# A two-layer AdaLN transformer stack on one core: where ScalarE's function tables are asked for, and a new order of the steps and idle matmuls of its two streams

## The chip, the cores and the metric

The kernel runs on 1 of the 8 cores of one Trainium2 chip. The metric is the device time of one execution in microseconds (us), lower is better; the number compared is the median of several executions. Engines: PE is TensorE, ACT is ScalarE, DVE is VectorE, POOL is GpSimd, and SP (SyncE) issues every DMA.

## The reference, cut to what matters

Eight sequences of 256 tokens with 128 features pass through two blocks, each with an attention part and a feed-forward part; each part gets `layernorm(x) * (1 + c) + s` and is added to `x` behind a gate.

```
x += ga * L0_attn(h)  # 8 heads of 64; an indexer picks 96 of 128 keys per half; Exp, Ln
x += gb * L0_ffn(h)   # two layers: windowed attention (l2norm, softmax) and a Gelu MLP of 341
x += ga * L1_attn(h)  # 16 heads of 8 over 256 keys; softmax
x += gb * L1_ffn(h)   # 16 experts, top 8 by a sigmoid router, one shared expert; Silu
```

All arithmetic is float32 but for the one-hot gathers, which are bf16 products.

## The kernel before

Sequences are worked on in pairs: stream 0 has sequences 0, 2, 4, 6 and stream 1 has 1, 3, 5, 7, four rounds each. Each engine has one Python generator per stream (`tensor_stream`, `scalar_stream`, `vector_stream`, `pool_stream`, `sync_stream`), cut into steps by `yield`. A step is mostly one wait on a semaphore and the few instructions that it releases. The two generators of an engine are merged into one instruction queue by a string of `STEPS_IN_TURN`: each character is a number in base 36, so many steps of one stream, the next character so many of the other, in turn. An engine works off its queue in order, so a step that waits holds up all behind it, of both streams.

`BUSY` has one string per stream, with a base-36 digit for each call of `keep_busy` in `tensor_stream`: so many idle matmuls (bf16, 128 columns of weights by 256, line L530, on the constant `mean_mat`) go ahead of the wait there, into a PSUM region whose contents are not needed. They compute nothing.

ACT needs a function table. Exp and Ln share one table set (`LN_AND_EXP`), Gelu and Silu have others; Copy, Identity, Square, Relu and Abs run with any. `table(act, name)` (L1149 to L1156) issues a load if the name differs from the last name asked for in build order: `preload_act_table_set` (L1153) for Ln and Exp, `preload_act_table` (L1155) for Gelu and Silu. Before the change a step function asks once, as a rule at the end of the step that precedes the one that uses the table, so ahead of a `yield`; between the asking and the use the string may place steps of the other stream. If the table that is then resident lacks the function of an activation, the compiler puts a load of its own right ahead of it; the trace lists such a load under the line of the activation (L1412 is the Exp of windowed attention, L1465 the Exp of the 16-head attention, L1519 the Silu of the experts).

Other lines named below: L616 the transposes of the probabilities (they wait for `u_prob`, which DVE sends after L1567 or L1570), L795 the down products of the experts, L2027 the product of Silu and up part on DVE, L1782 the cast that sends `top_ready`, L456 and L458 the saves of the picked indices, L467 their broadcast back to all partitions into `idxb`, L474 and L482 the save and the return of the gathered scores, L490 the store of the output.

Of the kernel before, what the change touches and what calls it, by code (L numbers as in the profile page):

```python
# [49 lines left out]
def shape_constants():  # L50
# [47 lines left out]
    "pe": ("922122242242e26437657223435346132423112621738272f3a16124132a5c6525522g83c2a9a4632a3c2a62281622232224241112221212"  # L98
            "3341135152514113315421252525252322235172663764314223236349143432249481c3a5226223622837254a3a161241525234c5c48362"
            "2837254a481228232224241112221212334113515231213112415411133215252523222351726637821243422123334934326435a4c3a3a1"  # L100
            "612415282c4a5226223622837254a5248362283c2a6127122823222424111222121233411351525151312231253515252523222252726637"
            "6532662372341734579381c3a4216423622w1628224322142421522z0i837252a62281622232224241112221212334113411231213112114"
            "5153d"),
    "act": ("d27253411927554275536143217325233323134311226132642184322823354581123226523431246822342622354622332g42e453333113"
            "5153552374c555552j573213423553416496262236434122911275541523221325534a43228253147862243325534741142h42e453333113"
            "51235233237452721145552j57454235b4633143285343634334327584322825334a61323221325534781224332543124622322h42e45333"
            "31135153722353545575552i411745423553415433752422368422712285543426132i222112452486222r53125534522332g42e45334442"
            "35236592c"),
    "dve": ("z0e4f69445494a4a79341444545412711436143315643163419221117252165518422164381521557174225951155917422a315541442121"
            "2mz082335e5385b375c358256441351e311b4c7834144454568415391544d123917424222112531557164127252165514452264182531557"  # L110
            "1641283411454144422mz131835c3228l355c358256441351d4a4f7834144494541245371641943421535174725216551a21251111623315"
            "21557164122752531557184312153111454144422mz0813153321a125354119365c358256441351c4b4f7834144454465113311436184491"
            "63917422521234121q5655214452122z0125114571542141631554144422mr131533c55385l"),
    "pool": ("gg11hhii44i243731m11hhii44e2838p11hhii44k2238p11hh922g744823339"),
    "sp": ("6211261131422611314226113142282"),
}
BUSY = [("a0g0v10000000000000000200b0010j00000000000500a00408000030d000140448000003000000000000000004006001b0001a780000630"
         "001000049f000063013000404480000030000000030000600000035g200000a70000000000000a000a0000630b0000404480000006000000"
         "03000010100006000b0091a701000000000001000000000301370e0000000006"),
        ("000000q00b00000000000400010000f03004063000000a006400000300351e0000000000030000e0097000e0020003080000a00000000000"  # L120
         "80000a002d80000301370e0000000000030001e0000000090000030001000203j000063090000a004240000301370e0006000000030004e0"
         "000000e00000030b0000o1k3l000000000500o1k3l5000848f00004044800000")]
# [170 lines left out]
def program(nc, A, out, idx_scratch, score_scratch):  # L293
    ctx = ExitStack()
    with ctx:
# [862 lines left out]
        def scalar_stream(act, st, s):  # L1158
# [12 lines left out]
            def ln_rstd(n):  # L1171
                table(act, LN_AND_EXP)
                yield
                act.wait_ge(*at("ln_var", n + 1))
                last_ = st.mark(act.activation(m.rstd, bank[2][:, 0:L], ACT.Ln, bias=eps_col[:, :]))
                yield
                st.wait(last_)
                act.activation(m.rstd, m.rstd, ACT.Exp, scale=-0.5).then_inc(*one("ln_rstd"))
# [7 lines left out]
            def query_parts(k):  # L1186

                q_abs, q_mu = m.q_tmp[k][0:2]
                raw = bank[3][:, H * DC:]
                table(act, LN_AND_EXP)  # L1190
                yield
                act.wait_ge(*at("q2_mm", k + 1))
                if k == 1:
                    act.wait_ge(*at("isummed", 1))
                last_ = st.mark(act.activation(q_abs, raw, ACT.Abs))
                yield
                st.wait(last_)
                last_ = st.mark(act.activation(q_abs, q_abs, ACT.Exp, scale=-1.0))
                yield
                st.wait(last_)  # L1200
                act.activation(q_mu, raw, ACT.Relu)
                act.activation(q_abs, q_abs, ACT.Ln, bias=one_col[:, :]).then_inc(*one("q2_log"))
                lat = bank[3][:, 0:256].rearrange("p (h n) -> p h n", h=H)
                copy(m.qa[k][:, :, 0:DC], lat)
                copy(m.qb[k][:, :, 0:DC], lat).then_inc(*one("q_latent"))
# [48 lines left out]
            def rescale(l, k):  # L1254
                table(act, LN_AND_EXP)
                yield
                act.wait_ge(*at("ssq_ready", 2 * l + k + 1))
                last_ = st.mark(act.activation(rs[s][:, k, :], ssq[s][:, k, :], ACT.Ln, scale=LN_SHIFT))
                yield
                st.wait(last_)  # L1260
                act.activation(rs[s][:, k, :], rs[s][:, k, :], ACT.Exp, scale=-0.5, bias=shift_col[:, :]).then_inc(*one("rs_ready"))
# [11 lines left out]
            for r in range(ROUNDS):  # L1273
# [24 lines left out]
                table(act, LN_AND_EXP)  # L1298
# [4 lines left out]
                yield  # L1303
                act.wait_ge(*at("kr_abs", 1))
                last_ = st.mark(act.activation(m.kr_abs, m.kr_abs, ACT.Exp, scale=-1.0))
                yield
                st.wait(last_)
# [29 lines left out]
                for i in range(6):  # L1337
                    yield
                    if i == 5:
                        act.wait_ge(*at("xg_turned", 1))  # L1340
                        act.wait_ge(*at("pdiag_zero", 1))
                        for t in range(GP):
                            part = slice(RANKS * t, RANKS * t + RANKS)
                            ins = copy(m.pdiag[part, :, t, :], bank[1][part, 0:H * NG].rearrange("p (h j) -> p j h", j=NG))
                        ins.then_inc(*one("pdiag_ready"))
                    if i >= 2:
                        u = i - 2
                        yield
                        act.wait_ge(*at("u_pv", u + 1))
                        copy(m.oTa[:, u % 2, cols(u // 2)], bank[3][:, 0:P]).then_inc(*one("u_out"))  # L1350
                    if i < 4:
                        T, half = i // 2, i % 2
                        table(act, LN_AND_EXP)
                        yield
                        act.wait_ge(*at("u_bias", i + 1))
                        for h in range(4):
                            probs = m.probs_a[T][:, 4 * half + h, :]
                            ins = act.activation(probs, probs, ACT.Exp, bias=nb[s][:, i, h:h + 1], scale=SCALE_A,  # L1358
                                                 accum_out=ls[s][:, i, h:h + 1])
                        ins.then_inc(*one("u_exp"))  # L1360
                    if 0 < i < 4:
                        yield
                    if 0 < i < 5:
                        yield from turned_out(0, i - 1, m.PTa[(i - 1) % 2])
                    yield
# [8 lines left out]
                for l in range(2):  # L1374
                    table(act, LN_AND_EXP)
# [16 lines left out]
                    for i in range(6):  # L1392
# [10 lines left out]
                        if i < 4:  # L1403
                            T, half = i // 2, i % 2
                            n = keys(T)
                            table(act, LN_AND_EXP)
                            yield
# [18 lines left out]
                    table(act, ACT.Gelu)  # L1426
                    for c in range(3):
                        n = HC[c]
                        yield
                        if c != 1:  # L1430
                            act.wait_ge(*at("f_g", 2 * l + 1 + c // 2))
# [23 lines left out]
                for v in range(4):  # L1455
                    yield
                    if v == 2:
                        act.wait_ge(*at("x_pv", 1))
                        copy(m.o1[:, 0:L], bank[0][:, 0:L]).then_inc(*one("x_o"))
                        yield  # L1460
                    table(act, LN_AND_EXP)
                    yield
                    act.wait_ge(*at("st_mm", v + 1))
                    for q in range(4):
                        act.activation(m.PT1[v][:, q, :, :].rearrange("p j n -> p (j n)"), bank[q], ACT.Exp, scale=SCALE_1)\  # L1465
                           .then_inc(*one("st_exp"))
                        if q == 1:
                            yield
                yield
                act.wait_ge(*at("x_pv", 2))  # L1470
                copy(m.o1[:, L:], bank[0][:, 0:L]).then_inc(*one("x_o"))
                yield
                table(act, LN_AND_EXP)
                yield
                act.wait_ge(*at("x_sum", 1))
                last_ = st.mark(act.activation(m.rs1, bank[1], ACT.Ln))
                yield
                st.wait(last_)
# [5 lines left out]
                yield  # L1484
                table(act, LN_AND_EXP)
                yield
# [3 lines left out]
                table(act, ACT.Silu)  # L1490
                copy(m.x_res, bank[3][:, P:3 * P].rearrange("p (k n) -> p k n", k=NT))
                copy(m.gate_row, bank[3][:, 3 * P:]).then_inc(*one("x_res"))
                yield
                act.wait_ge(*at("e_gate", 1))
                act.activation(m.moe_g[:, 0:L], bank[0][:, 0:L], ACT.Silu).then_inc(*one("e_silu"))
                yield
                for i in range(1, 6):
# [14 lines left out]
                    if i < 5:  # L1512
                        table(act, ACT.Silu)
                        for j in range(2):
                            yield
                            act.wait_ge(*at("e_gate", 2 * i + j))
# [767 lines left out]
```

## Time and profile before

| | |
|---|---|
| median of 3 runs | 1498.68 us (1488.72 to 1499.29) |
| the profiled execution | 1503.2 us, its span 1501.4 us |
| busy: PE, DVE, ACT, POOL | 1292.5, 900.6, 897.6, 362.2 us (86, 60, 60, 24%) |
| mean granted TensorE clock | 0.950 |

The span goes from the first to the last instruction; 1.8 us of the profiled time lie around it. Busy time of PE includes the idle matmuls.

### The profile page before, as it was taken

What the parts mean: (1) busy time and instruction counts of PE and PEld (TensorE: products, weight loads), DVE (VectorE), ACT (ScalarE), POOL (GpSimd) and SP (SyncE); (2) the same over time, 40 slices, a digit from 0 to 9 for tenths busy, and PEclk for the clock granted to TensorE, in tenths of its full rate; (3) what the DMA queues carried; (4) which work ended last, traced back from release to release, by engine and by line L of the source; (5) the groups of instructions that cost most, each with busy time, mean ns of one, the idle gap of its engine ahead of it and who ended that gap; (6) DMA issues with size and microseconds to landing.
All of it is one profiled execution on the core that took longest, in us unless ns stands there. A gap on an engine that the chain in (4) does not pass through costs nothing.

```text
span 1501.4 us, 31001 instructions
## 1 busy us (share of the span) xinstructions
PE 1292.5 (86%) x11954; PEld 914.2 (61%) x11954; DVE 900.6 (60%) x2920; ACT 897.6 (60%) x2256; POOL 362.2 (24%) x580
## 2 busy tenths in 40 slices
PE   7788988879887998988898988887899798988887
PEld 5455655657764665656665655665676566656566
DVE  3966665553776666663476566756367566656533
ACT  3435676647843677747673567764785356665463
POOL 0601242000450222210153023310036123040003
PEclk8898999999999999999998999999999989999999
DMA  8120000000022000000012100000002200000000
GB/s 281 51 77 13 2 1 1 1 5 4 5 65 76 4 2 1 1 1 4 8 47 70 28 2 1 1 1 5 5 5 64 71 10 2 1 1 1 1 1 8
DMA packets 31795, 34.90 MB, mean 23 GB/s; under 512 B 19168, under 2 KB 23712, under 8 KB 31136
## 3 DMA queue, kind: packets, MB, share of 16 engines
q1 hardware_dynamic: 31648, 32.92, 7.4%
q8 instruction: 95, 1.56, 0.4%
q14 instruction: 52, 0.43, 0.1%
HBM read 25.46 MB, written 7.44 MB: 22 GB/s over the span
## 4 chain that ended last, share of the span: by engine, by line
PE 56%; ACT 21%; DVE 14%; issue 3%; DMA 3%; POOL 2%; SPq 2%; POOLq 0%; DVEq 0%; ACTq 0%
ACT arena L1412 4%; PE ps L530 4%; PE ps L557 4%; PE ps L795 4%; ACT arena L1164 4%; DVE small L1953 3%; PE ps L728 3%; ACT L1153 2%; PE ps L687 2%; PE ps L1069 2%; PE ps L616 2%; PE ps L1052 2%; PE ps L772 2%; PE ps L780 2%; PE ps L657 2%
## 5 line engine op out<-in xcount | busy, mean ns | idle before, releaser
L1164 ACT ACTIVATE arena<-ps 128x512 f32<-128x512 f32 (+7 forms) x560 | 258.6, 483 | 283.2 <-PE ps L580 39.1
L530 PE MATMUL ps<-mean_mat 128*128 128x256 bf16 x1120 | 157.0, 282 | 19.9 <-ACT arena L1164 10.1
L2101 POOL TENSOR_TENSOR arena<-arena 128x512 f32<-128x512 f32 x64 | 80.8, 1272 | 313.7 <-DVE arena L1604 312.4
L530 PEld LDWEIGHTS ps<-mean_mat 128*128 128x128 bf16 x1120 | 107.7, 101 | 63.2 <-issue 29.3
L1412 ACT ACTIVATE arena<-arena,small 128x128 f32<-128x128 f32 (+1 forms) x256 | 129.7, 509 | 13.2 <-DVE small L1890 12.8
L1579 DVE CUSTOM_DVE_ANT_0 arena<-ps,mask_w_bf 128x128 f32<-128x128 f32 (+1 forms) x256 | 67.5, 319 | 64.3 <-PE ps L671 63.8
L1953 DVE TENSOR_REDUCE small<-ps 128x4 f32<-128x1024 f32 x64 | 75.5, 1220 | 30.2 <-PE ps L1052 29.7
L795 PE MATMUL ps<-w_experts,arena 128*128 128x128 f32 x544 | 77.1, 299 | 11.2 <-DVE arena L2027 11.0
L795 PEld LDWEIGHTS ps<-w_experts,arena 128*128 128x128 f32 x544 | 71.6, 210 | 24.0 <-issue 11.8
L2027 DVE TENSOR_TENSOR arena<-arena,ps 128x512 f32<-128x512 f32 x64 | 43.0, 686 | 71.4 <-ACT arena L1519 40.2
L1358 ACT ACTIVATE arena<-arena,small 128x224 f32<-128x224 f32 (+1 forms) x128 | 56.3, 444 | 42.1 <-DVE small L1838 42.1
L1465 ACT ACTIVATE arena<-ps 128x512 f32<-128x512 f32 x128 | 66.3, 601 | 25.2 <-PE ps L1088 25.1
L557 PE MATMUL ps<-hot_ring,arena 128*96 128x512 bf16 x192 | 58.0, 447 | 23.8 <-DVE gath L1814 21.7
L1814 DVE TENSOR_TENSOR gath<-ps,rank_tab 96x512 f32<-96x512 f32 x96 | 62.8, 681 | 25.2 <-PE ps L557 18.0
L1567 DVE TENSOR_TENSOR arena<-arena,small 128x512 f32<-128x512 f32 x96 | 70.6, 736 | 2.8
L2186 POOL TENSOR_TENSOR arena<-arena 128x256 f32<-128x256 f32 x32 | 24.1, 754 | 196.8 <-ACT arena L1507 194.9
L772 PE MATMUL ps<-arena,w_experts 128*128 128x256 f32 x272 | 69.3, 397 | 0.0
L780 PE MATMUL ps<-arena,w_experts 128*128 128x256 f32 x272 | 66.1, 383 | 1.7 <-ACT arena L1507 1.5
L728 PE MATMUL ps<-w_wqkv,arena 128*128 128x512 f32 x128 | 62.5, 631 | 3.7 <-DVE arena L1557 3.7
L616 PE MATMUL ps<-packed,arena 128*128 128x128 f32 x384 | 62.9, 288 | 3.0 <-DVE arena L1570 1.3
L1579 DVE CUSTOM_DVE_ANT_0 arena<-ps,mask_a_bf,small 128x192 f32<-128x192 f32 (+1 forms) x128 | 41.6, 381 | 38.6 <-PE ps L603 38.2
L1507 ACT ACTIVATE arena<-ps,arena 128x128 f32<-128x128 f32 x128 | 36.5, 371 | 46.3 <-PE ps L795 46.3
(291 smaller groups left out, 2965.9 us busy)
## 6 DMA issues: line engine op xcount, KB each, us to landing
idxb<-idx_scratch SPq DMA_DIRECT2D x24, 512.0 KB, 5.3
score_scratch<-arena SPq DMA_DIRECT2D x96, 64.0 KB, 1.7
w_experts<-in_experts SPq DMA_DIRECT2D x3, 1088.0 KB, 16.3
w_wqkv<-in_wqkv SPq DMA_DIRECT2D x1, 1536.0 KB, 9.4
arena<-score_scratch SPq DMA_DIRECT2D x96, 16.0 KB, 2.0
arena<-in_x SPq DMA_DIRECT2D x8, 128.0 KB, 2.2
out_x<-arena SPq DMA_DIRECT2D x8, 128.0 KB, 1.8
packed<-in_packed SPq DMA_DIRECT2D x2, 503.0 KB, 4.0
```

The costliest lines, as they stand in the source:

```text
L530: mm(to, still[:, 0:P], still, start=True, stop=True)
L557: last = mm(bank[g % 2][0:GF, :], m.kv_part[i][:, 0, :], hot[n][:, part], start=(i == 0), stop=(n < 2 and i == 2))
L616: last = pe.transpose(bank[2][:, cols(h)], probs[:, h, :], ident[:, :])
L728: mm(bank[2 * k + j], m.sh[:, cols(k)], wqkv[:, l, 512 * j:512 * j + 512], start=True, stop=True)\
L772: last = mm(bank[j // 2][:, L * (j % 2):L * (j % 2) + L], experts[:, 0, e, :], m.hT, start=True, stop=True)
L780: last = mm(to[:, L * (j % 2):L * (j % 2) + L], experts[:, 1, e, :], m.hT, start=True, stop=True)
L795: last = mm(bank[2 + j // 2][:, 256 * (j % 2) + P * k:256 * (j % 2) + P * k + P], m.moe_h[:, L * j + P * k:L * j + P * k + P], experts[:, ...
L1164: return act.activation(dst, src, ACT.Copy)
L1412: ins = act.activation(probs, probs, ACT.Exp, bias=nb[s][:, i, h:h + 1], scale=cqs[s][:, T, hh_:hh_ + 1], accum_out=ls[s][:, i, h:h + 1])
L1579: ins = dve.tensor_tensor_reduce(masked[:, h, 0:n], bank[h % 2][:, n * (h // 2):n * (h // 2) + n], mask, 1.0, least(h), ALU.add, ALU.max, ...
L1953: st.mark(dve.tensor_reduce(to, src, AX.X, ALU.max))
L2101: ins = pool.tensor_tensor(own, own, turned, ALU.add)
```

## The change

Three things are changed. `table` is asked for in each step that uses it, behind that step's `yield` and ahead of its wait, and again in each later step of the same function. The strings of `STEPS_IN_TURN` are new for all five engines (the steps themselves and their number are the same: 2138 on PE, 1841 on ACT, 2410 on DVE, 560 on POOL, 82 on SP). The strings of `BUSY` are new.

```diff
-    "pe": ("922122242242e26437657223435346132423112621738272f3a16124132a5c6525522g83c2a9a4632a3c2a62281622232224241112221212"
+    "pe": ("821112244222g26437677323236617321212244113t1a3a5841528171a455a4632a372a4522362121d672a15222846222112222424411212"
...
-    "act": ("d27253411927554275536143217325233323134311226132642184322823354581123226523431246822342622354622332g42e453333113"
+    "act": ("d212437327322a9274312464634322162623338122m23338262536488223426223348327221b27223345522ef33321313343545523344421"
...
-    "sp": ("6211261131422611314226113142282"),
+    "sp": ("621126113131112611314226113142282"),
...
-BUSY = [("a0g0v10000000000000000200b0010j00000000000500a00408000030d000140448000003000000000000000004006001b0001a780000630"
+BUSY = [("b0h50z000000000010003000050475004000000000000000000000b00000000i0000000000000000000000001000300005020000c0000000"
...
             def ln_rstd(n):
+                yield
                 table(act, LN_AND_EXP)
-                yield
                 act.wait_ge(*at("ln_var", n + 1))
                 last_ = st.mark(act.activation(m.rstd, bank[2][:, 0:L], ACT.Ln, bias=eps_col[:, :]))
                 yield
+                table(act, LN_AND_EXP)
                 st.wait(last_)
...
-                            table(act, LN_AND_EXP)
                             yield
+                            table(act, LN_AND_EXP)
                             act.wait_ge(*at("u_bias", 4 * l + i + 5))
...
-                    table(act, ACT.Gelu)
                     for c in range(3):
                         n = HC[c]
                         yield
+                        table(act, ACT.Gelu)
...
                         if q == 1:
                             yield
+                            table(act, LN_AND_EXP)
...
-                table(act, ACT.Silu)
                 copy(m.x_res, bank[3][:, P:3 * P].rearrange("p (k n) -> p k n", k=NT))
                 copy(m.gate_row, bank[3][:, 3 * P:]).then_inc(*one("x_res"))
                 yield
+                table(act, ACT.Silu)
...
-                        table(act, ACT.Silu)
                         for j in range(2):
                             yield
+                            table(act, ACT.Silu)
```

The same move is made in `query_parts`, `rescale`, the front (`kr_abs`), the softmax of the first attention, `x_rs` and the router.

## Rows read from the trace of the kernel before

**Rows 1.** The page: the chain that ended last, shares of the span by engine.

```profile
PE 56%; ACT 21%; DVE 14%; issue 3%; DMA 3%; POOL 2%; SPq 2%; POOLq 0%; DVEq 0%; ACTq 0%
```

**Rows 2.** The chain by line, shares; then its first and last table load (start, us).

```profile
by line: ACT arena L1412 4.4%; PE ps L530 4.1%; PE ps L557 4.0%; PE ps L795 3.8%; ACT arena L1164 3.6%; issue 3.2%; DVE small L1953 2.8%; PE ps L728 2.7%; ACT L1153 2.5%; PE ps L687 2.3%; PE ps L1069 2.2%; PE ps L616 2.2%; PE ps L1052 2.1%;
...
196.42 1.28 ACT L1155
...
1456.38 1.28 ACT L1153
```

**Rows 3.** Groups by line, ACT: count, busy us, mean ns, idle before.

```profile
L1155 ACT ACT_TABLE_LOAD x44 | 56.5, 1283 | 0.8
L1153 ACT ACT_TABLE_LOAD x43 | 55.2, 1283 | 0.8
L1412 ACT ACT_TABLE_LOAD x5 | 6.4, 1283 | 0.1
L1465 ACT ACT_TABLE_LOAD x3 | 3.8, 1283 | 0.1
L1519 ACT ACT_TABLE_LOAD x3 | 3.8, 1283 | 0.1
```

**Rows 4.** The chain in order of time (start, us), experts beside 16-head attention.

```profile
344.93 1.28 ACT L1155
...
346.23 0.60 ACT arena L1519
...
346.84 1.28 ACT L1465
...
348.13 1.08 ACT arena L1465 x2
...
349.24 1.28 ACT L1519
...
352.00 3.76 PE ps L795 x16
...
362.33 1.98 PE ps L795 x16
```

**Rows 5.** Groups by line, PE: the idle matmuls.

```profile
L530 PE MATMUL ps<-mean_mat 128*128 128x256 bf16 x1120 | 157.0, 282 | 19.9 <-ACT arena L1164 10.1 <-ACT arena L1243 6.0 <-DVE arena L1589 3.8
```

**Rows 6.** The chain, last round: packs of idle matmuls (start, us).

```profile
1276.68 2.79 PE ps L530 x24
...
1286.16 2.40 PE ps L530 x21
...
1329.24 5.29 PE ps L530 x24
```

**Rows 7.** Instructions of DVE in order of time, beside those packs.

```profile
1276.71 0.69 DVE L1567 TENSOR_TENSOR arena<-arena,small 128x512 f32<-128x512 f32 x1
...
1287.32 0.42 DVE L1570 TENSOR_TENSOR arena<-arena,small 128x256 f32<-128x256 f32 x1
...
1327.81 1.75 DVE L1567 TENSOR_TENSOR arena<-arena,small 128x512 f32<-128x512 f32 x1
```

**Rows 8.** Windows: stretch, length, busy of PE, PEld, DVE, ACT, POOL; clock, DMA.

```profile
345.50:352.30 6.80, 3.76 (x28) 2.76 (x27) 1.38 (x2) 6.71 (x8) 0.00 (x0) 0.93 0.01 2
352.30:359.20 6.90, 6.90 (x27) 6.25 (x27) 1.22 (x4) 5.58 (x12) 0.72 (x1) 0.57 0.00 0
```

**Rows 9.** Instructions in order of time: DVE's cast, SP's queue, round 1.

```profile
443.67 0.18 DVE L1782 CAST arena<-arena 128x64 bf16<-128x64 uint32 x1
...
444.42 2.47 SPq L482 DMA_DIRECT2D arena<-score_scratch  x4
446.93 1.58 SPq L456 DMA_DIRECT2D idx_scratch<-arena  x1
...
450.27 1.29 SPq L467 DMA_DIRECT2D idxb<-idx_scratch  x3
```

**Rows 10.** SP's queue: output stores and later broadcasts.

```profile
808.19 1.29 SPq L467 DMA_DIRECT2D idxb<-idx_scratch  x3
...
783.72 0.39 SPq L490 DMA_DIRECT2D out_x<-arena  x1
...
1142.50 0.39 SPq L490 DMA_DIRECT2D out_x<-arena  x1
```

More of the change, by code:

```diff
@@ L97 @@
 STEPS_IN_TURN = {
-    "pe": ("922122242242e26437657223435346132423112621738272f3a16124132a5c6525522g83c2a9a4632a3c2a62281622232224241112221212"
[L99 to L103, printed above, removed]
@@ L104 @@
-    "act": ("d27253411927554275536143217325233323134311226132642184322823354581123226523431246822342622354622332g42e453333113"
[L105 to L113, printed above, removed]
@@ L114 @@
-    "pool": ("gg11hhii44i243731m11hhii44e2838p11hhii44k2238p11hh922g744823339"),
-    "sp": ("6211261131422611314226113142282"),
-}
-BUSY = [("a0g0v10000000000000000200b0010j00000000000500a00408000030d000140448000003000000000000000004006001b0001a780000630"
[L118 to L122, printed above, removed]
+    "pe": ("822112244222g26437677323236617321212244113t1a3a5841528171a455a4632a372a4522362121d672a15222846222112222424411212"
+            "221212212132115142113111123125531224212523272221217272643767732323661732121224411221f1c1a2a5841528171a3611281612"
+            "31225151a452a1a1612413272a45252512282824272211123212222231114211515251511122212515152525232222527266376773232366"
+            "17321212245321z021218282112229482c1k1612413272a351a321818413272a452525122828232224141122121232431152515142115111"
+            "2221251515252523222252726236855743234349141222231112312231a1c3c584632a371a5558425682c3c1816222352h672f1a28232624"
+            "21121222121221111211211341134115351515335"),
@@ new lines @@
+    "act": ("d212437327322a9274312464634322162623338122m23338262536488223426223348327221b27223345522ef33321313343545523344421"
+            "35a2235442182c5542a52464634322162623338142i22231382625364a22111282421132228252322a21334822332l42j433445351536233"
+            "421134553233352j573212311234312464634322162623338142n2332222364f2a2322a21334d422322623334822332g321332g321134153"
+            "53546233421134553233352l55321342b43564433328233334623152a2335822172322334882224162723353317h46223a2lf43423333445"
+            "2334253a225"),
@@ new lines @@
+    "dve": ("t4o1b89645494c4369441444544652431e341441p361c41c571c442395117571744236134a1c5715412541444242412ju151335c35583523"
+            "85d3m9213833434b4e44681331144321443652471d311441h3d1d41c591e4325416541a442a2521855174429311531553134123j1112z091"
+            "51431c328335c365b833256411351d4d4c78341444544652431e341441v37164591444111k25218551747111645216551744293115414541"
+            "32122i1214z0d111431c328335c365b823356411351b4f4ca814449458123415391544c113b1e45a17571942239531c5e164541f442a3716"
+            "45413412432jj2731c22135g38558"),
@@ new lines @@
+    "pool": ("d3251811hhii44e5858k11hhii44l2138p11hhii44j233721n11hhii4458366"),
+    "sp": ("621126113131112611314226113142282"),
+}
+BUSY = [("b0h50z000000000010003000050475004000000000000000000000b00000000i0000000000000000000000001000300005020000c0000000"
+         "0000050000000000000b000i0300000000c0000000000000100030000501b393000000000000060000000000000b03094308000000c00000"
+         "000000000040010000001003c0000000000000003c0000000900000700500000"),
+        ("003800500000000000000300000000140a0000000030600000000000003000000000000098g0005000000000000000000000001000000000"
+         "0000060000000003d900000000000000009000e0000000000000000005000002d0000000000006000000000300800f000000000000900080"
+         "010000c000000000000000000a00050000506006000000030036000000000000")]
@@ L1254, in rescale @@
             def rescale(l, k):
+                yield
                 table(act, LN_AND_EXP)
-                yield
                 act.wait_ge(*at("ssq_ready", 2 * l + k + 1))
@@ L1259, in rescale @@
                 yield
+                table(act, LN_AND_EXP)
                 st.wait(last_)
@@ L1297, in scalar_stream @@
                 act.activation(m.kr_abs, rope, ACT.Abs).then_inc(*one("kr_abs"))
-                table(act, LN_AND_EXP)
                 yield
@@ L1303, in scalar_stream @@
                 yield
+                table(act, LN_AND_EXP)
                 act.wait_ge(*at("kr_abs", 1))
@@ L1306, in scalar_stream @@
                 yield
+                table(act, LN_AND_EXP)
                 st.wait(last_)
@@ L1352, in scalar_stream @@
                         T, half = i // 2, i % 2
+                        yield
                         table(act, LN_AND_EXP)
-                        yield
                         act.wait_ge(*at("u_bias", i + 1))
@@ L1374, in scalar_stream @@
                 for l in range(2):
-                    table(act, LN_AND_EXP)
                     yield from key_squares(l, 0)
@@ L1405, in scalar_stream @@
                             n = keys(T)
+                            yield
                             table(act, LN_AND_EXP)
-                            yield
                             act.wait_ge(*at("u_bias", 4 * l + i + 5))
@@ L1460, in scalar_stream @@
                         yield
+                    yield
                     table(act, LN_AND_EXP)
-                    yield
                     act.wait_ge(*at("st_mm", v + 1))
@@ L1468, in scalar_stream @@
                             yield
+                            table(act, LN_AND_EXP)
                 yield
@@ L1472, in scalar_stream @@
                 yield
+                yield
                 table(act, LN_AND_EXP)
-                yield
                 act.wait_ge(*at("x_sum", 1))
@@ L1477, in scalar_stream @@
                 yield
+                table(act, LN_AND_EXP)
                 st.wait(last_)
@@ L1484, in scalar_stream @@
                 yield
+                yield
                 table(act, LN_AND_EXP)
-                yield
                 act.wait_ge(*at("route_mm", 1))
```

## The prediction

> **What bounds the kernel now.** I read the chain that ended last first, by engine [rows 1]: PE has 56% of it, ACT 21%, DVE 14%, so no engine is the bound for long. The end is set by a thread that crosses from engine to engine, in two interleaved streams that share in-order queues. PE is busy 86% of the span, but part of that is idle matmuls. Next the chain by line [rows 2]: the reader is to see two things in it that compute nothing, the idle matmuls (L530, 4.1%, of 1501.4 us 61.6) and the table loads (L1153 alone 2.5%). Then the groups by line, for the number of both [rows 3, 5]; then the chain in order of time where such loads and packs stand thick, and the other engines beside them, to see when the data for the next real instruction were there [rows 4, 6, 7]; last the granted clock, since fewer matmuls could lower it [rows 8].
>
> **Table loads.** Steps of the merged queues can be counted from the strings alone. Walked through with the old string and the old places, ACT asks for a change of name 87 times (43 Ln/Exp, 16 Gelu, 28 Silu), and 11 times an activation finds the wrong table: a Gelu or Silu of one stream was placed between the asking and the Exp of the other. The trace has just these: 43 and 44 loads at the two lines of `table`, and 5 + 3 + 3 = 11 of the compiler's own [rows 3], 98 in all. The three loads of the start-up are not touched. Walked with the new string and the new places it is 79 changes of name (39 Ln/Exp, 16 Gelu, 24 Silu), and no activation finds the wrong table, which it can't, since the asking stands in the same step. So 98 - 79 = 19 loads go, each 1.283 us: 24.4 us of ACT's time.
>
> What of that is on the path? The chain has 62 loads, the first and last of them in [rows 2], 62 x 1.283 = 79.6 us. All 11 of the compiler's own are among them. That is plain at the experts: Silu load, Silu, Exp load, two Exp, Silu load, Silu, with nothing idle between [rows 4], ACT busy 6.71 of 6.80 us and PE only 3.76 [rows 8]. The same happens in rounds 0, 1 and 2. In the new string the four Exp stand together, then both Silu: two loads fewer each time, 2.6 us of a path on which the down products L795 wait. The 51 others on the chain are 59% of the 87 asked for. If 59% of the new 79 stay on it, 46.6 x 1.283 = 59.8 us are left, and 79.6 - 59.8 = 19.8 us go. I take **-20**. The bounds: all 19 on the path, -24.4; or all 79 left come onto it, because a load now stands in the queue behind the other stream's steps instead of ahead of them and finds less idle time to hide in, 79 x 1.283 = 101.4, which is +21.8. I stay near the first, since the load still stands ahead of its step's own wait, so what hides it is that wait; it is exposed where the releaser is already there when ACT comes to it. The repeated asking costs nothing: with the name unchanged no instruction is issued. One ask moves past work: the router's Silu load now comes behind the two copies that send `x_res`, so PE gets those 1.28 us earlier and the Silu no later.
>
> Behind a load the trace shows no further pause: load at 344.93 for 1.28, Silu at 346.23 [rows 4]. The Trainium skill (ScalarE: Activation LUTs, "What ACT_TABLE_LOAD costs") has the same 1283 ns, but adds a drain of about 1380 ns to each switch, some 2.66 us; by that the 19 loads would be an estimated 50 us and the sum about 26 us more. The rows are against the drain, and the sum doesn't use it.
>
> **Idle matmuls.** The digits of `BUSY` sum to 483 + 637 = 1120, as the trace has [rows 5], and the new ones to 347 + 265 = 612. Their busy time is 157.0 us for 1120, 140 ns each, so 508 fewer take 71 us off PE. 61.6 us of L530 are on the chain, and by count 508/1120 of it, 27.9 us, goes. But a pack on the chain isn't all loss: behind it real work would have waited for its data. The last round shows how much. In stream 1 a pack of 24 ends at 1279.47 [rows 6] and the data for L616 were there at 1277.40 [rows 7]: 2.07 us too long of 2.79. The pack of 21 ends at 1288.56, the data at 1287.74: 0.82 of 2.40. The pack of 24 at 1329.24, at the lower clock, ends at 1334.53, the data were there at 1329.56: 4.97 of 5.29. The same stream and round has the largest cut, 252 to 74. On the other hand many packs of 8 or less are shorter than the wait they stand in. Half of 27.9 is **-14**; the bounds are 0 (every gap is filled by waiting) and -27.9.
>
> **SP and the orders.** In SP's queue one thing changes: in round 1 the saves of stream 1's indices (L456, L458) come ahead of the return of stream 0's scores (L482), not behind. The cast that releases them ended at 443.85, the saves were issued from 446.93, behind four L482 of 2.47 us, and the broadcast L467 at 450.27 [rows 9], all on the chain. In the new order the saves are issued at 443.9 to 445.1, land as the L482 (now 0.7 us later) are issued, and L467 starts at about 447.6: **-2.5** for stream 1, while stream 0's scores come 0.7 us later. Rounds 0, 2 and 3 keep their order. POOL moves a handful of steps between rounds (expert sums of stream 1 against the rotary products of stream 0), of which POOL, busy 24%, has room for; I count 0, at worst one such operation, 1.3 us, in each of four rounds.
>
> The new orders of PE, ACT and DVE have no price in the trace of before, as they are hundreds of exchanges. The nearest rows are what the orders of different rounds, which differ from each other as well, give: in stream 1 from broadcast to output store 333.5 us (450.27 to 783.72) in round 1 and 334.3 (808.19 to 1142.50) in round 2 [rows 9, 10]. Orders that differ in detail are worth about 1 us a round. From that I take **0**, and +-10 for four rounds; an order that was made for other load places can be worth more in both directions, which is in the range.
>
> **Clock.** The mean granted clock is 0.950, so a tenth of the span, 150 us, runs at the lower level, 1.2 GHz, the rest at 2.4. What a lower stretch costs: 16 L795 take 3.76 us in one and 1.98 at full [rows 4]; in 3.4 us of PE's work on the path 1.7 is lost. It fell at 352.3 after PE had stood still for 3 of 6.8 us, because ACT was loading tables [rows 8]; this recurs in three rounds, and these falls should go or become shorter, at best 3 x 3.4 = 10 us. Against that stand gaps that packs no longer fill. I let the two cancel: **0**, with -10 to +68 (next part).
>
> The sum: 20 + 14 + 2.5 = 36.5 us. Against the profiled execution's own 1503.2 us that is 1466.7. It lay 4.5 us above the median of the runs shown, so the median after should be 1498.7 - 36.5 = **1462 us** (-2.4%).
>
> **The rivals.**
> (a) The clock. Fewer idle matmuls leave PE idle in the softmax stretches, and the clock falls more often. 73 fewer places have a pack (162 to 89). Were there 20 more lower stretches of 6.9 us, at 3.4 us each, that is 68 us lost against 36.5 gained: 1530 us, slower. It decides from 11 more such stretches, a mean clock of about 0.92. For it speaks that the clock fell after PE's idle time in [rows 8]; against it, that it fell there in spite of a full set of packs, and that the pack at 1329.24 ran at the lower clock itself [rows 6]. The Trainium skill (TensorE: Matmul & The Clock Gate, "HAM oscillation — how this bites in real kernels") holds that idle PE brings the half clock, which speaks against this cut of packs; the rows agree on the direction. Chance 0.10.
> (b) What goes is hidden anyway. The two streams share the queues, so that a us saved in one is spent waiting for the other; exposed loads and the new orders' own waits take over. Then only part of the 11 loads that were surely on the path is gained: 8 to 10 us, 1490 us. For it speaks that the chain goes over to another engine at nearly every step, 14% of it DVE [rows 1]. Also here: that the new strings don't fit the real durations. Chance 0.17.
> (c) All of it counts: 24.4 of loads, 27.9 of idle matmuls, 2.5 of SP, and 3 of the orders and the clock, 58 us: 1441; with an order that also fills PE's gaps down to 1425. PE's real work is only 1292.5 - 157.0 = 1135.5 us, so there is room. Chance 0.15.
> (d) The forecast, 0.58.
>
> **How the numbers follow.** About 1% is what a measurement of this kernel can tell from no change; the three runs shown lie 10.6 us apart. Faster by over 1% are (d) and (c), 0.73; (b) is 0.17 within 1%; (a) is 0.10. The range goes from 1428, which cuts off the end of (c), to 1500, which takes in (b) with its spread and leaves (a) out.
>
> **What would show it.** In the profile after: loads only at the two lines of `table`, 79 of them, none under an Exp or Silu line; at the experts four Exp in a row, and L795 about 2.6 us sooner; L530 x612, with about 85 us busy and 2 to 3% of the chain; L467 of round 1 ahead of the time above by 2.5 us; a mean clock of 0.94 to 0.96. A clock under 0.92 makes (a) right. A chain where L1153 and L1155 have more than 5% means that the loads came into the open. If L530 halves and the span doesn't move, (b) is right, and the waits of PE should have grown by the same amount.

## The result, and the profile after

The kernel after takes 1414.46 us (median of 4 runs, 1412.24 to 1414.97) against 1497.66 us of the kernel before: a ratio of 0.945, 95% interval 0.942 to 0.948, so 83 us or 5.5% less. The forecast was 1462 us, with a range of 1428 to 1500: the sign was right, the size less than half. The profiled execution has a span of 1412.1 us and a mean granted clock of 0.968; a clock given for an experiment below is that of its profiled execution.

The page of the kernel after: span, busy us and instructions, then the chain by engine ([rows 1] before).

```profile
span 1412.1 us, 29992 instructions
PE 1221.4 (86%) x11446; PEld 850.2 (60%) x11446; DVE 905.8 (64%) x2920; ACT 868.7 (62%) x2237; POOL 362.2 (26%) x580
PE 53%; ACT 19%; DVE 16%; issue 4%; DMA 3%; POOL 2%; SPq 1%; DVEq 0%; POOLq 0%; ACTq 0%
```

The groups of the kernel after that answer to [rows 3] and [rows 5]:

```profile
L1155 ACT ACT_TABLE_LOAD x40 | 51.3, 1283 | 0.7
L1153 ACT ACT_TABLE_LOAD x39 | 50.0, 1283 | 0.7
...
L530 PE MATMUL ps<-mean_mat 128*128 128x256 bf16 x612 | 88.0, 287 | 15.3 <-ACT arena L1164 11.7 <-DVE arena L1594 2.6 <-DVE arena L1636 1.1
```

The counts are the forecast ones: 79 loads, none of the compiler's own in the streams, 612 idle matmuls. What was not forecast is how little of the loads is left on the chain. Its lines, and the first and last of the 32 pieces of it that are table loads ([rows 2] before):

```profile
by line: ACT arena L1415 5.2%; PE ps L795 4.1%; ACT arena L1164 4.0%; PE ps L557 3.6%; issue 3.6%; PE ps L780 3.4%; PE ps L772 3.4%; PE ps L728 3.2%; ACT arena L1468 2.4%; DVE small L1958 2.3%; PE ps L1069 2.1%; DMA idxb<-idx_scratch 2.1%; 
...
191.62 1.28 ACT L1155
...
1311.21 1.28 ACT L1153
```

L530 and L1153 are gone from the head of the list. Added up over the whole chain, idle matmuls are 25.5 us (62.0 before) and table loads 39.2 us in 32 pieces (78.6 us in 62 before; some are on it only in part). At the experts the chain now reads (start, us; [rows 4] before):

```profile
329.90 1.28 ACT L1153
...
331.68 1.57 ACT arena L1468 x3
...
333.27 1.28 ACT L1155
...
334.57 0.61 ACT arena L1524
...
336.63 2.02 PE ps L795 x16
```

The four Exp (one of them just ahead of the x3) stand together, then the Silu. To compare like with like, start at the Exp load ahead of the first of the four; before, that is one row above those of [rows 4]:

```profile
342.53 1.27 ACT L1153
```

From there to the down products L795 it is 9.5 us before (342.53 to 352.00, four loads) and 6.7 us after (329.90 to 336.63, two loads): 2.7 us less, two loads of 1.283 us and hardly more. These L795 run at the full level, 2.02 us instead of 3.76. The L795 of rounds 1 and 2 behind the same two Silu go from the lower level to the full one too. Two rows of before, then two of after:

```profile
707.16 3.76 PE ps L795 x16
...
1069.11 3.75 PE ps L795 x16
```

```profile
679.82 1.98 PE ps L795 x16
...
1018.28 2.02 PE ps L795 x16
```

So the falls of the clock at the experts, which the prediction said should go or become shorter, are gone in all three rounds (the granted clock is 1.00 also from 671 to 685 us and from 1018 to 1032 us). The windows of round 0 (columns as in [rows 8]):

```profile
330.00:337.00 7.00, 5.58 (x39) 4.53 (x40) 2.38 (x6) 6.93 (x10) 0.00 (x0) 1.00 0.01 2
337.00:344.00 7.00, 7.00 (x63) 5.39 (x63) 1.82 (x5) 6.95 (x13) 0.73 (x1) 1.00 0.06 17
```

**A ledger of PE.** Span = real work of PE + idle matmuls + gaps of PE. Each is one subtraction on the page: PE busy less the busy time of the L530 group is real work, span less PE busy is gaps. Before: 1292.5 - 157.0 = 1135.5 real, 157.0 idle matmuls, 1501.4 - 1292.5 = 208.9 gaps. After: 1133.4, 88.0, 190.7. Of the 89.3 us, 69.0 are idle matmuls and 18.2 are gaps. The surprise is the last: 69 us of filling were taken out and the gaps did not grow, they shrank.

**By round.** SP's queue, kernel after, shows the broadcasts of stream 1 and the output stores (start, us; [rows 9, 10] before):

```profile
430.10 1.48 SPq L467 DMA_DIRECT2D idxb<-idx_scratch  x3
...
749.15 0.39 SPq L490 DMA_DIRECT2D out_x<-arena  x1
...
775.05 1.30 SPq L467 DMA_DIRECT2D idxb<-idx_scratch  x3
...
1088.55 0.39 SPq L490 DMA_DIRECT2D out_x<-arena  x1
...
1113.61 1.29 SPq L467 DMA_DIRECT2D idxb<-idx_scratch  x3
```

Broadcast to store in stream 1 is 319.0 and 313.5 us where it was 333.5 and 334.3. From one broadcast to the next it is 345.0 and 338.6 us (before 357.9 and 358.0), and from the last to the end 298.5 (before 335.2). Every round gains, the last one most.

### The profile page after: what moved, and what is told of

It reads as the page before. It is cut to its first block, busy times and chain, and to the rows that moved or that the text cites. A ratio compares the mean times of both kernels' runs of the same rounds, so it can differ in the third digit from the quotient of the medians.

```text
span 1412.1 us, 29992 instructions
## 1 busy us (share of the span) xinstructions
PE 1221.4 (86%) x11446; PEld 850.2 (60%) x11446; DVE 905.8 (64%) x2920; ACT 868.7 (62%) x2237; POOL 362.2 (26%) x580
## 4 chain that ended last, share of the span: by engine, by line
PE 53%; ACT 19%; DVE 16%; issue 4%; DMA 3%; POOL 2%; SPq 1%; DVEq 0%; POOLq 0%; ACTq 0%
ACT arena L1415 5%; PE ps L795 4%; ACT arena L1164 4%; PE ps L557 4%; PE ps L780 3%; PE ps L772 3%; PE ps L728 3%; ACT arena L1468 2%; DVE small L1958 2%; PE ps L1069 2%; DMA idxb<-idx_scratch 2%; PE ps L657 2%; PE ps L530 2%; PE ps L1052 2%; PE ps L1088 2%
## 5 line engine op out<-in xcount | busy, mean ns | idle before, releaser
L530 PE MATMUL ps<-mean_mat 128*128 128x256 bf16 x612 | 88.0, 287 | 15.3 <-ACT arena L1164 11.7
L530 PEld LDWEIGHTS ps<-mean_mat 128*128 128x128 bf16 x612 | 58.8, 102 | 41.5 <-issue 16.6
L795 PEld LDWEIGHTS ps<-w_experts,arena 128*128 128x128 f32 x544 | 64.3, 191 | 26.8 <-issue 15.2
L795 PE MATMUL ps<-w_experts,arena 128*128 128x128 f32 x544 | 69.1, 279 | 12.5 <-DVE arena L2032 7.8
L780 PE MATMUL ps<-arena,w_experts 128*128 128x256 f32 x272 | 65.5, 381 | 0.0
L772 PE MATMUL ps<-arena,w_experts 128*128 128x256 f32 x272 | 65.3, 379 | 0.0
L1512 ACT ACTIVATE arena<-ps,arena 128x128 f32<-128x128 f32 x128 | 36.7, 373 | 35.7 <-PE ps L795 35.1
L1584 DVE CUSTOM_DVE_ANT_0 arena<-ps,mask_a_bf,small 128x192 f32<-128x192 f32 (+1 forms) x128 | 41.6, 380 | 25.9 <-PE ps L603 25.5
```

The lines of the kernel that those rows point to most:

```text
L530: mm(to, still[:, 0:P], still, start=True, stop=True)
L772: last = mm(bank[j // 2][:, L * (j % 2):L * (j % 2) + L], experts[:, 0, e, :], m.hT, start=True, stop=True)
L780: last = mm(to[:, L * (j % 2):L * (j % 2) + L], experts[:, 1, e, :], m.hT, start=True, stop=True)
L795: last = mm(bank[2 + j // 2][:, 256 * (j % 2) + P * k:256 * (j % 2) + P * k + P], m.moe_h[:, L * j + P * k:L * j + P * k + P], experts[:, ...
L1584: ins = dve.tensor_tensor_reduce(masked[:, h, 0:n], bank[h % 2][:, n * (h // 2):n * (h // 2) + n], mask, 1.0, least(h), ALU.add, ALU.max, ...
```

## The experiments

Theories. **A**: what goes from the queues makes the gain, loads and idle matmuls each by themselves; the order is worth little (the forecast's view). **B**: the new order makes the gain. Later **C**: what counts of an idle matmul is where it stands, not how many there are. The change has three parts that can be exchanged freely: the asks (code of `scalar_stream`), the strings of `STEPS_IN_TURN`, the strings of `BUSY`. Ratios are to the kernel before.

**e1, the asks alone.**

```diff
-                            table(act, LN_AND_EXP)
                             yield
+                            table(act, LN_AND_EXP)
```
(and all other asks of the change; both sets of strings as before)

> Old order and old idle matmuls, only the asking for tables moved into the steps: 93 loads in the streams instead of 98, none of the compiler's own. Theory A (what goes from the queues makes the gain, the order itself little): 5 loads of 1.283 us, all on the path, ratio to the kernel before about 0.996; Theory B (the new order makes most of the gain): the same, 0.995 to 1.00. If loads come into the open because they now stand behind the other stream's steps: over 1.005.

Ratio 0.998 (0.995 to 1.001), 93 loads. In the old order that part is worth nothing that these runs can tell: the old string puts Exp steps of one stream between Gelu or Silu steps of the other, so most of what the compiler loaded must now be asked for. 60 of the 93 loads are on this chain, 76.0 us.

**e2, the idle counts alone.**

```diff
-BUSY = [("a0g0v10000000000000000200b0010j000...
+BUSY = [("b0h50z000000000010003000050475004...
```

> Old order and old asks, only the new counts of idle matmuls (612 instead of 1120). Theory A: most of the 62 us of idle matmuls on the chain that fall to 25 us in the kernel after are given back here too, ratio 0.975 to 0.985. Theory B: the counts fit only the new order; here waits take their place, 0.99 to 1.00. Clock theory: the granted clock falls under 0.93 and the ratio is over 1.00.

Ratio 1.016 (1.010 to 1.023), clock 0.932: **slower**. Theory A falls here. The page of e2 and its group of idle matmuls:

```profile
span 1514.8 us, 30011 instructions
PE 1252.4 (83%) x11446; PEld 880.3 (58%) x11446; DVE 897.1 (59%) x2920; ACT 897.7 (59%) x2256; POOL 362.8 (24%) x580
```

```profile
L530 PE MATMUL ps<-mean_mat 128*128 128x256 bf16 x612 | 88.4, 288 | 6.2 <-ACT arena L1164 6.0 <-DVE arena L1589 0.2
```

69 us of idle matmuls less, gaps 262.4 instead of 208.9, real work 1164.0 instead of 1135.5 at the lower clock.

**e3, asks and idle counts, old order** (both edits above).

> New asks and new idle counts in the old order. Theory A: about 0.97, that is over half of the 5.5%. Theory B: 0.985 to 0.995, with over two thirds of the gain missing.

Ratio 1.019 (1.012 to 1.026), clock 0.924. Without the new order the change makes the kernel slower.

**e4, the order alone.**

```diff
-    "pe": ("922122242242e26437657223435346132423112621738272f3a16124132a5c6525522g83c2a9a4632a3c2...
+    "pe": ("821112244222g26437677323236617321212244113t1a3a5841528171a455a4632a372a4522362121d672...
```
(and the strings of the four other engines)

> Only the new strings of steps; asks and the 1120 idle matmuls as before, whose counts now stand at places that they were not made for. 79 asked loads and 12 of the compiler's own. Theory A: near 1.00 (0.985 to 1.01), since the idle matmuls and nearly as many loads are still there. Theory B: 0.95 to 0.97.

Ratio 1.012 (1.008 to 1.016). B falls as well, in its plain form: the order alone doesn't bring it either. Idle matmuls (L530) have 5.9% of this chain, 89 us.

**e5, the kernel after with the old idle counts; e6, the kernel after with the old asks** (the edits of e2 and e1 taken back).

> The kernel after with the old counts of idle matmuls (1120). Theory A: the 508 idle matmuls cost 35 us or more again, ratio to the kernel before 0.97. Theory B: ratio 0.95 to 0.96, as most of them fall into waits.

> The kernel after with the asks at their old places: 79 asked loads and 12 of the compiler's own. Theory A: 12 loads of 1.283 us on the path, 15 us, ratio 0.955. Theory B: under half of that comes through, 0.945 to 0.95.

e5: 0.998 (0.995 to 1.001), so the old counts cost 0.053, 79 us, in the new order. In its profiled execution, at 1510.6 us the longest of ten, L530 has 6.0% of the chain, and packs of 24, 20 and 21 are again among the longest on it. e6: 0.961 (0.957 to 0.965), so the asks are worth 0.016, 24 us, in the new order. My count of 12 own loads of the compiler was short: the trace has 20. Instructions of ACT in e6, in order of time:

```profile
729.18 1.28 ACT L1198 ACT_TABLE_LOAD   x1
730.47 0.42 ACT L1198 ACTIVATE arena<-arena 128x256 f32<-128x256 f32 x1
...
731.31 1.28 ACT L1202 ACT_TABLE_LOAD   x1
732.61 0.51 ACT L1202 ACTIVATE arena<-arena,one_col 128x256 f32<-128x256 f32 x1
```

L1198 is an Exp and L1202 the Ln after it. The set that the compiler picks for the first lacks the second, so a missed ask costs two loads in such a pair. Not every load is exposed: 13 of the 20, 16.7 us, are on the chain of e6. All table loads together have 59.0 us of it, where the kernel after has 39.2; that is 19.8 of the 24 us.

**e7 and e8, no idle matmul at all, in the kernel after and before.**

```diff
-BUSY = [("b0h50z000...
+BUSY = [("000000000...
```

> The kernel after with no idle matmul at all. If idle matmuls only cost: 25 us of them are on its chain, ratio to before 0.93. If they hold the clock up: the granted clock falls from 0.968 to under 0.94 and the ratio is 0.95 or more.

> The kernel before with no idle matmul. If idle matmuls only cost: up to the 62 us that they have on its chain go, ratio 0.96. If the order holds the time: 0.98 to 0.99 with waits in their place. If they hold the clock up: clock under 0.92 and the ratio over 1.00.

e7: 0.969 (0.965 to 0.973), clock 0.938. e8: 1.015 (1.010 to 1.020), clock 0.915. Idle matmuls are worth their place in both, 36 us in the new order and 22 in the old. The pages of e8 and e7:

```profile
span 1521.8 us, 28830 instructions
PE 1220.2 (80%) x10834; PEld 844.3 (55%) x10834; DVE 897.0 (59%) x2920; ACT 897.6 (59%) x2256; POOL 361.9 (24%) x580
```

```profile
span 1444.7 us, 28811 instructions
PE 1193.9 (83%) x10834; PEld 823.2 (57%) x10834; DVE 902.3 (62%) x2920; ACT 867.4 (60%) x2237; POOL 360.3 (25%) x580
```

**e13 and e14 close the square without idle matmuls**: new order with old asks, old order with new asks.

> New order, asks at the old places, no idle matmul. With old order it was 1.015 (e8), with new asks 0.969 (e7). Theory order: the order carries it, 0.98. Theory asks: 12 loads on the path carry a good part, 0.99 or more.

> Old order, new asks, no idle matmul. Theory order: as e8, 1.01 to 1.015. Theory asks: 0.99 to 1.00.

| no idle matmul | old asks | new asks |
|---|---|---|
| old order | 1.015 (e8) | 1.020 (e14; 1.014 to 1.025) |
| new order | 0.988 (e13; 0.983 to 0.992) | 0.969 (e7) |

The order alone is worth 0.027, 41 us, and the asks, once the order is there, 0.019, 28 us. With the idle matmuls of each order on top (36 and 22 us, e7 and e8) this path adds up to the result: 41 + 28 + 36 - 22 = 83 us. On another path the shares are others (e1 to e6), since the parts aren't independent. The page of e13:

```profile
span 1479.2 us, 28831 instructions
PE 1218.8 (82%) x10834; PEld 839.5 (57%) x10834; DVE 901.9 (61%) x2920; ACT 895.3 (61%) x2257; POOL 360.8 (24%) x580
```

From e8 to e13 PE's real work is the same (1220.2, 1218.8), and its gaps fall from 301.6 to 260.4: what the order does is fit the streams into each other. From e13 to e7 the gaps fall by 9.6 only, but real work by 24.9, with the clock up from 0.923 to 0.938. On the chain, table loads fall from 73.1 us (57 of them) to 43.1 (35).

**e9 and e10, every idle count of the kernel after doubled and halved.**

```diff
-                for _ in range(int(next(busy), 36)):
+                for _ in range(2 * int(next(busy), 36)):
```
(e10: `int(next(busy), 36) // 2`)

> The kernel after with every count of idle matmuls doubled (1224, more than the 1120 of before), at the same places. Theory C (what counts is where the packs stand: the old counts cost 79 us in the new order because they stand ahead of work whose data are there): 612 more at the right places cost far less than those, ratio to before 0.95 to 0.975. Theory A (number alone, 0.14 us each when exposed): 0.14 x 612 = 86 us, about 1.00.

> The kernel after with every count halved (277 left). With none the ratio was 0.969, with all 0.945. If the packs work through the clock, half of them give about half, 0.955, with the clock between 0.938 and 0.968. If half of each pack was too much, 0.945 or below.

e9: 0.972 (0.965 to 0.979), clock 0.970. 612 idle matmuls more, at their places, cost 40 us; the 508 more of e5, at the places of another order, 79. That is theory C, though the number is not nothing. e10: 0.949 (0.942 to 0.955), clock 0.963, not told apart from the kernel after: 277 well placed ones do nearly all that 612 do. Its page and its group of idle matmuls:

```profile
span 1416.5 us, 29330 instructions
PE 1191.7 (84%) x11111; PEld 823.4 (58%) x11111; DVE 906.0 (64%) x2920; ACT 867.8 (61%) x2237; POOL 362.1 (26%) x580
```

```profile
L530 PE MATMUL ps<-mean_mat 128*128 128x256 bf16 x277 | 45.9, 284 | 15.5 <-ACT arena L1164 11.9 <-DVE arena L1594 2.6 <-DVE arena L1636 1.1
```

Against the kernel after, 42.1 us of idle matmuls are gone, the gaps are 34.2 us longer (224.9) and real work 12.4 us (1145.8): what is given up and what is gained cancel.

**e16, every idle count of the kernel before halved** (the `// 2` of e10, in the kernel before).

> The kernel before with every count of idle matmuls halved (518 left), at its own places. If the number is what matters, as with the 612 of e2: 1.015. If the place is: 0.995 to 1.005, between the packs that are too long and the clock.

Ratio 0.998 (0.995 to 1.001), with 518, where e2 with 612 had 1.016: in the old order too it is the place. A plain cut in the old order isn't told from no change. Its page and group:

```profile
span 1489.1 us, 29805 instructions
PE 1241.5 (83%) x11352; PEld 862.7 (58%) x11352; DVE 904.0 (61%) x2920; ACT 898.8 (60%) x2256; POOL 363.1 (24%) x580
```

```profile
L530 PE MATMUL ps<-mean_mat 128*128 128x256 bf16 x518 | 86.3, 289 | 20.3 <-ACT arena L1164 9.1 <-ACT arena L1243 6.9 <-DVE arena L1589 4.3
```

**e11 and e12, the strings cut at round 3.** All five orders and both `BUSY` strings are cut where stream 0 starts its round 3 on PE (804 and 773 PE steps of the two streams, in the old order 804 and 775) and joined with the rest of the other kernel's; asks new.

```diff
-    "pe": one kernel's string
+    "pe": its first 804 and 773 steps, then the other kernel's order of all later steps
```

> Order and idle counts of the kernel after up to the start of stream 0's round 3, from there those of before; new asks. In the kernel after the last round is 37 us shorter, the three before it 13 to 21 us each. If each round's order and counts work by themselves: 37 us of the 83 are missing, ratio 0.97. If the gain hangs on the whole string: 0.98 to 1.00.

> The other half: before's order and counts up to stream 0's round 3, then those of after; new asks. If rounds work by themselves: 37 us are gained, ratio 0.975. If the last round was only short because the rounds before it left it a better start: 0.99 to 1.00.

e11: 0.969 (0.963 to 0.976); e12: 0.979 (0.972 to 0.986). The two parts multiply to 0.949: rounds work by themselves, 31 us in the last, 46 in the three before it. Windows of the L530 group alone, last round (from stream 1's broadcast to the end), kernel before and then after (stretch, length, PE busy, PEld busy, clock, DMA):

```profile
1166.20:1501.40 335.20, 45.69 (x331) 31.78 (x331) 0.94 0.04 11
```

```profile
1113.60:1412.10 298.50, 17.29 (x122) 11.00 (x122) 0.98 0.04 12
```

The round is 36.7 us shorter, and PE has 28.4 us less of idle matmuls in it.

**e15, SP's order taken back.**

```diff
-    "sp": ("621126113131112611314226113142282"),
+    "sp": ("6211261131422611314226113142282"),
```

> The kernel after with the order of before on SP alone: one exchange in round 1. By the prediction 2.5 us slower than the kernel after, ratio to before 0.947; if hidden, 0.945. In the trace the broadcast of stream 1 in round 1 shows it, at 430.1 in the kernel after.

Ratio 0.951 (0.947 to 0.956), where the kernel after has 0.945 (0.942 to 0.948): the intervals overlap, so the whole time can't tell 2.5 us from nothing. The place can. SP's queue in e15, then in the kernel after:

```profile
415.97 1.74 SPq L474 DMA_DIRECT2D score_scratch<-arena  x4
...
427.79 0.60 SPq L456 DMA_DIRECT2D idx_scratch<-arena  x1
...
430.15 1.29 SPq L467 DMA_DIRECT2D idxb<-idx_scratch  x3
...
706.06 0.38 SPq L490 DMA_DIRECT2D out_x<-arena  x1
```

```profile
418.05 1.74 SPq L474 DMA_DIRECT2D score_scratch<-arena  x4
...
426.26 0.48 SPq L456 DMA_DIRECT2D idx_scratch<-arena  x1
...
430.10 1.48 SPq L467 DMA_DIRECT2D idxb<-idx_scratch  x3
...
707.44 0.38 SPq L490 DMA_DIRECT2D out_x<-arena  x1
```

The broadcast starts at nearly the same time, 430.15 and 430.10, but that comparison misleads: up to the exchange the two kernels are the same, and yet the two executions already lie 2.08 us apart at the first L474 shown. From that L474 to the broadcast it is 14.18 us without the exchange and 12.05 with it, 2.1 us less. With it the chain comes to the broadcast no longer from the saves but from PE (kernel after; start, us), for which it stands 0.4 us:

```profile
429.36 1.12 PE ps L588 x16
430.49 0.14 SPq L467
```

At the next output store (706.06 and 707.44) the executions are 1.38 us apart, so 0.7 of the 2.1 us are left there.

## Why the prediction was wrong, point by point

**The step that failed** is "The new orders of PE, ACT and DVE ... From that I take **0**, and +-10 for four rounds". Measured without idle matmuls and with the old asks, the order is worth 41 us (e8 to e13). The reasoning compared rounds 1 and 2, which agree to 1 us. But both are stretches of one string, made together; that they agree doesn't tell what a string made anew can do. The rows for a bound were there: PE's gaps of 208.9 us, and the last round, where idle matmuls, 331 of both streams, filled 45.7 us (e11). The room was named in case (c) ("so there is room") and not priced.

**Adding up terms failed too.** The sum treated the three parts as independent. They aren't: asks are worth 24 us in the new order (e6) and 4, within the noise, in the old (e1); the idle counts +24 us in the old order (e2) and -79 in the new (e5 to after). Asks and counts together, without the order, make 1.019 (e3).

**Idle matmuls: -14, by half of the part of the chain that goes by count.** The size was off, and so was the picture. Against no idle matmuls, with the ledger: in the old order 157.0 us of them took 92.7 us of gaps (301.6 to 208.9), so 64.3 us stood in the way, and real work fell by 84.7 us with the clock up from 0.915 to 0.950. In the new order 88.0 us took 60.1 of gaps, 27.9 in the way, and real work fell by 60.5. What stands in the way fell by 36.4 us, which is what the chain says (62.0 to 25.5). By this reckoning the packs on the chain of before were nearly all overrun, that is, ran on beyond the moment when the data were there; the three packs worked out in the prediction had said 7.86 of 10.48 us, and I halved them without a row for it. And a part of the good that the old packs did was given up. Net the counts are worth 36 against 22 us: 14 us more, by accident the number forecast, but only together with the order; alone they cost 24.

**Table loads: -20.** The count was right. Removed from the chain were 39.3 us, of which the number explains 24.4 at most. The rest is that of the 79 left 32 are on the chain (39.2 us, some only in part) where 59%, 46.6, were assumed. That is the order's doing: with the same asks and the old idle counts 60 of 93 are on it in the old order (e1) and 25 of 79 in the new (e5). The bound "+21.8", loads coming into the open behind the other stream's steps, didn't happen: 0.998 in e1. At the experts what was forecast, 2.6 us, is seen: 2.7. No pause stands behind a load: in the kernel before the next instruction of ACT starts within 0.03 us in 89 of 101 cases, in the kernel after in 68 of 82 (start-up included; in e6, load at 729.18 for 1.28, Exp at 730.47). The Trainium skill (ScalarE: Activation LUTs, "What ACT_TABLE_LOAD costs") adds a drain of about 1380 ns to each switch. The traces don't agree with that, as the prediction held.

**SP: -2.5.** The mechanism was right at its place: the broadcast comes 2.1 us sooner behind the same work (e15), then held for 0.4 us by PE, which the prediction didn't ask about. By the next output store 0.7 us are left. What it is worth in the whole time these runs can't tell.

**The clock: 0.** The clock rose to 0.968, and real work of PE is 2.1 us shorter (1133.4). The falls at the experts went as forecast. Rival (a) was not what happened in this kernel, but its mechanism is real: 612 idle matmuls in the old order bring 0.932 and a loss of 1.6%. The cut of packs did no harm in the order that leaves fewer gaps. The Trainium skill (TensorE: Matmul & The Clock Gate, "HAM oscillation — how this bites in real kernels") holds that PE's waiting brings the half clock. The mean clocks of e7, e8 and e2 agree in direction: 0.938, 0.915 and 0.932, each with more gaps on PE than the kernel of the same order with its own idle matmuls (0.968 and 0.950).

Rival (c), given 0.15, had the right direction, 1441 and "down to 1425"; it came out 10 us below even that.

**Still open**: which exchanges within the PE, ACT and DVE strings make the 41 us. They can't be had apart by exchanging one engine's string alone: in the kernel after, PE's, ACT's, DVE's or POOL's old order with the new ones of the others waits in a circle, by the semaphores. No run has such a mix.

## What to carry to other kernels

Where two streams share in-order queues, an order, the filling (here idle matmuls) that stands in its gaps and the placing of set-up work (here table loads) are one design: each of them taken over alone was worth nothing or cost up to 1.6%, together they gave 5.5%. Before two executions are compared by start times, line them up at an instruction ahead of the change (e15). Bound what a new order can give by the gaps of the busiest engine and by what filling overruns there, not by how alike the old order's rounds are. Filling is judged by its place: measure how late the data of the instruction behind each pack come, and count the part beyond it as cost. Ask for a table in the step that uses it, and let the order keep uses of one table together.

## What the runs showed of the hardware that was not expected

A table load that the compiler places ahead of an Exp or Ln doesn't serve both: in e6 an Exp and the Ln behind it got a load each, 1.283 us twice (729.18 and 731.31), where the asked set serves both with one. Idle matmuls pay for themselves through the clock to a degree that I had not expected: 157 us of them shortened 1220 us of real work on PE to 1135.5, with the granted clock going from 0.915 to 0.950. But 277 of them do as much as 612 (0.949 and 0.945, intervals overlapping).
